# Output projection of an attention block: twelve of sixteen token tiles by Strassen's seven block products

## The reference, cut to what matters

```python
x = L0_attn_hidden_states                       # 4 x 512 tokens, 1024 channels
xn = _layernorm(x, axis=-1)
s = _L0_attn_ref(xn, Wq, Wk, Wv, Wo)            # 16 heads of 64, causal; its last line:
#   return out @ Wo                             #   out: 2048 x 1024, Wo: 1024 x 1024
g = _silu(_L0_ffn_ref(xn, weight, bias, gate_w, in_channel_scale, out_channel_scale))
x = x + s * g                                   # what is returned
```

## Time and profile before

| What | Value |
|---|---|
| Median of 3 runs | 1167.71 us (1166.72 to 1168.52) |
| The profiled execution: its own time | 1166.3 us |
| Its span, from the first to the last instruction | 1164.5 us |
| Mean granted TensorE clock | 0.994 |
| PE busy over the span | 1132.8 us (97%) |
| Wo's matmuls of tiles 4 to 15 | 12 x 48 = 576, about from 1028 to 1159 us |

### The profile page before, as it was taken

One profiled execution on the slowest core, in us unless ns is written; L12 is line 12 of the kernel. 1 busy time (PEld: TensorE's weight loads), 2 busy tenths in 40 slices (PEclk: granted clock), 3 DMA queues, 4 the chain that ended last, 5 costly groups with the idle time before them and its releaser, 6 DMA issues.

```text
span 1164.5 us, 17720 instructions
## 1 busy us (share of the span) xinstructions
PE 1132.8 (97%) x5692; PEld 945.4 (81%) x5692; DVE 727.5 (62%) x1731; ACT 611.7 (53%) x1286; POOL 424.5 (36%) x254
## 2 busy tenths in 40 slices
PE   4899999999999999999999999999999999999998
PEld 3677777788888888888888888888888887888886
DVE  6757741477767777677676776767767678323222
ACT  6545543266655666656665566655666577312211
POOL 0433537343342433424334252342523434222221
PEclk9899999999999999999999999999999999999999
DMA  9425132220202202022360220202202034565662
GB/s 368 192 91 235 55 91 109 73 64 10 63 9 72 63 9 63 9 72 63 144 216 9 72 63 9 63 9 72 63 9 63 9 112 168 172 204 179 193 207 99
DMA packets 87271, 112.01 MB, mean 96 GB/s; under 512 B 3408, under 2 KB 68944, under 8 KB 86224
## 3 DMA queue, kind: packets, MB, share of 16 engines
q1 hardware_dynamic: 87248, 111.72, 28.9%
HBM read 78.15 MB, written 33.55 MB: 96 GB/s over the span
## 4 chain that ended last, share of the span: by engine, by line
PE 88%; DVE 6%; ACT 2%; issue 1%; POOL 1%; DMA 1%; SPq 0%; DVEq 0%; POOLq 0%; ACTq 0%
PE at_proj L44 17%; PE at_proj L46 17%; PE at_proj L45 17%; PE at_out L978 7%; PE ff_z_ps L287 6%; PE at_pt L965 6%; PE at_score L947 3%; PE at_score L948 3%; PE at_score L44 3%; PE at_score L46 2%; PE at_score L45 2%; POOL ff_xs_lo L679 1%; PE at_proj L932 1%; DVE xs_full L600 1%; DMA z<-fn_in_channel_scale_dram 1%
## 5 line engine op out<-in xcount | busy, mean ns | idle before, releaser
L44 PE MATMUL at_proj<-xn_hi,w_hi 128*128 128x512 f32 x896 | 361.7, 404 | 1.6 <-POOL w_lo L1403 0.8
L46 PE MATMUL at_proj<-xn_hi,w_lo 128*128 128x512 f32 x896 | 350.9, 392 | 0.0
L45 PE MATMUL at_proj<-xn_lo,w_hi 128*128 128x512 f32 x896 | 349.4, 390 | 0.0
L46 PEld LDWEIGHTS at_proj<-xn_hi,w_lo 128*128 128x128 f32 x896 | 168.2, 188 | 37.3
L44 PEld LDWEIGHTS at_proj<-xn_hi,w_hi 128*128 128x128 f32 x896 | 168.5, 188 | 31.9 <-issue 1.2
L45 PEld LDWEIGHTS at_proj<-xn_lo,w_hi 128*128 128x128 f32 x896 | 168.8, 188 | 30.3
L1387 POOL TENSOR_TENSOR at_turning<-at_turning,rope_table 128x512 f32<-128x512 f32 x64 | 82.9, 1295 | 289.3 <-DVE at_turning L1231 289.3
L1395 POOL TENSOR_TENSOR w_lo<-w_stage,w_hi 128x1024 fp32r<-128x1024 f32 x45 | 114.4, 2557 | 162.9 <-ACT w_hi L1063 162.9
L1101 ACT ACTIVATE at_prob<-at_score,at_neg_max 128x512 f32<-128x512 f32 (+3 forms) x256 | 133.3, 526 | 71.2 <-DVE at_neg_max L1259 70.8
L1110 ACT ACTIVATE at_pt_hi<-at_pt 128x512 fp32r<-128x512 f32 (+1 forms) x192 | 94.0, 524 | 99.9 <-PE at_pt L965 99.1
L1276 DVE TENSOR_TENSOR at_pt_lo<-at_pt,at_pt_hi 128x512 fp32r<-128x512 f32 (+1 forms) x192 | 111.9, 597 | 42.2 <-ACT at_pt_hi L1110 41.2
(11 more groups left out here) (125 smaller groups left out, 1825.6 us busy)
## 6 DMA issues: line engine op xcount, KB each, us to landing
z_store<-z SPq DMA_DIRECT2D x16, 512.0 KB, 2.7
w_stage<-in_L_attn_Wq_dram SPq DMA_DIRECT2D x16, 512.0 KB, 3.8
w_stage<-in_L_attn_Wk_dram SPq DMA_DIRECT2D x16, 512.0 KB, 5.1
w_stage<-in_L_attn_Wv_dram SPq DMA_DIRECT2D x16, 512.0 KB, 6.2
att_store<-at_att_t SPq DMA_DIRECT2D x32, 256.0 KB, 2.0
rope_table<-att_store SPq DMA_DIRECT2D x16, 512.0 KB, 6.7
z<-_attn_hidden_states_dram SPq DMA_DIRECT2D x16, 512.0 KB, 5.0
at_turning<-z_store SPq DMA_DIRECT2D x16, 512.0 KB, 6.1
```

The costliest lines, as they stand in the source:

```text
L44: pe.matmul(out, sh, mh, start=first, stop=False)
L45: pe.matmul(out, sh, ml, start=False, stop=False)
L46: return pe.matmul(out, sl, mh, start=False, stop=final)
```

## The change

Tiles 0 to 3 stay as they are (`PLAIN = 4`). Tiles 4 to 15 are taken in six rounds of two tiles. In a round the two tiles' attention rows are a 2 x 2 matrix of blocks (A11, A12 from the even tile, A21, A22 from the odd one, each 128 tokens by 512 channels), and Wo is one as well (512 by 512 each). Seven block products, each of 4 x 3 = 12 matmuls, give the four output blocks, by way of sums: S1 = A21 + A22, S2 = S1 - A11, S3 = A11 - A21, S4 = A12 - S2 on the side of attention, and T1 to T4 of Wo's blocks. That is 84 matmuls in a round, where two tiles had 96.

What comes with it:

- **Before the rounds**: Wo is loaded a second time (`load_rows`, four loads of two rows of blocks, 512 KB each), DVE makes T1 to T4 from it (`sums`, 16 instructions), ACT makes high parts (`sums_high`, 16), DVE and POOL low parts (`sums_low`, 8 each).
- **In each round**: DVE makes the four sums of attention blocks (`row_sums`) and four low parts (`op_low`), POOL three low parts, ACT seven high parts (`op_hi`), all of 128x512. ACT copies a partial sum out of PSUM three times (`part_copy`), because bank a goes on accumulating for another output block; DVE adds three banks to those copies (`block_sum`), multiplies and adds x by halves (`block_out`, three times two), and `block_21` ends the round with the last product's bank.
- **Order**: TensorE's products in a round are P1 = A11 W11 (bank a), P2 = A12 W21 (bank b), P3 = S2 T2 (a), P4 = S1 T1 (c), P5 = S3 T3 (a), P6 = S4 W22 (c), P7 = A22 T4 (a). P3 waits for the copy of P1's bank, P5 for that of P3's, P6 for that of P4's, and P7 for `block_sum(q, 2)`, which reads bank a after P5. The next round has other banks.
- **Buffers**: the result is written over x (four places, `x_slots`), no longer into `y_tile`; the multiplication writes over z. `load_z` and `load_x` are apart, and the loads of z and of attention rows stand ahead of the next store in SP's queue.

The core of the diff:

```diff
+        sum_b = sb("at_sum_b", [P, 2, EMBED], F32)
+        wo_sum = [[sb(f"at_wo_sum{t}_{part}", [P, QT, HALF], F32R) for part in ("hi", "lo")] for t in range(4)]
+        a22 = sb("at_a22", [P, 2, HALF], F32R)
+        partial = sb("at_partial", [P, 3, HALF], F32)
...
-        x_tile = keep["z"]
+        x_slots = [keep["z"][:, p, :] for p in range(2)] + [keep["w_stage"][:, p, :] for p in range(2)]
         z_tile = turning[:].rearrange("p a b n -> p a (b n)")
-        y_tile = [prob[p][:, 0:EMBED] for p in range(2)]
+
+        wo_rows = [sum_b, keep["w_stage"][:, 0:2, :]]
+        att_sum = sum_b[:].rearrange("p a (b n) -> p (a b) n", b=2)
...
+        banks = [(pt_ps[0], pt_ps[1], out_ps), (proj_ps[0], proj_ps[1], score_ps[0])]
...
+            def load_rows(k):
+
+                if k == 0:
+                    sp.wait_ge(qk_ready, 2 * STEPS)
+                    sp.wait_ge(v_tr, STEPS)
+                    sp.wait_ge(scored, 6 * STEPS - 6)
+                elif k == 1:
+                    wait_wo(sp, 6)
+                    wait_wo(sp, 7)
+                else:
+                    sp.wait_ge(sum_low_dve, 2 * (k - 1))
+                    sp.wait_ge(sum_low_pool, 2 * (k - 1))
+                for half in range(2):
+                    rows = slice((QT * half + k) * P, (QT * half + k + 1) * P)
+                    sp.dma_start(wo_rows[k % 2][:, half, :], io["wo"][rows, :]).then_inc(rows_in[k % 2], 16)
...
+            load_rows(2)
+            store_y(0)
+            load_z(2)
+            load_att(4)
+            store_y(1)
+            load_z(3)
+            load_x(2)
+            load_x(3)
+            load_rows(3)
...
+            for n in range(PLAIN, TILES, 2):
+                store_y(n)
                 if n + 2 < TILES:
-                    load_att(n + 2)
-                sp.wait_ge(y_add, n + 1)
-                sp.dma_start(out[tile_rows(n), :], y_tile[n % 2]).then_inc(y_out[n % 2], 16)
+                    load_z(n + 2)
+                if n + 4 < TILES:
+                    load_att(n + 4)
+                    load_att(n + 5)
+                store_y(n + 1)
                 if n + 2 < TILES:
-                    load_xz(n + 2)
+                    load_z(n + 3)
+                if n + 4 < TILES:
+                    load_x(n + 4)
+                    load_x(n + 5)
...
+            def product(out, op, moving, first):
+                (sh, sl), (mh, ml) = operand(op), moving
+                for k in range(QT):
+                    last = split_matmuls(pe, out[:], (sh[:, k, :], sl[:, k, :]), (mh[k], ml[k]), first=(first and k == 0),
+                                         final=(k == QT - 1), reopened=not first)
+                last.then_inc(product_done, 1)
...
+                product(a, A11, wo_block(0, 0), True)
+                pe.wait_ge(op_low_pool, 3 * q + 2)
+                product(b, A12, wo_block(1, 0), True)
+                pe.wait_ge(op_low_dve, 4 * q + 1)
+                pe.wait_ge(sum_low_dve, 2 * QT - 1)
+                pe.wait_ge(partial_ok, 3 * q + 1)
+                product(a, S2, wo_sum_block(T2), False)
+                pe.wait_ge(op_low_dve, 4 * q + 2)
+                pe.wait_ge(sum_low_dve, 2 * QT)
+                product(c, S1, wo_sum_block(T1), True)
+                pe.wait_ge(op_low_dve, 4 * q + 3)
+                pe.wait_ge(sum_low_pool, 2 * QT - 1)
+                pe.wait_ge(partial_ok, 3 * q + 2)
+                product(a, S3, wo_sum_block(T3), False)
+                pe.wait_ge(op_low_dve, 4 * q + 4)
+                pe.wait_ge(partial_ok, 3 * q + 3)
+                product(c, S4, wo_block(1, 1), False)
+                pe.wait_ge(op_low_pool, 3 * q + 3)
+                pe.wait_ge(sum_low_pool, 2 * QT)
+                pe.wait_ge(block_read, 3 * q + 2)
+                product(a, A22, wo_sum_block(T4), False)
...
+            def part_copy(q, which):
+
+                act.wait_ge(product_done, 7 * q + (1, 3, 4)[which])
+                if q >= 1:
+                    act.wait_ge(block_done, 3 * (q - 1) + (1, 3, 2)[which])
+                act.activation(partial[:, which, :], banks[q % 2][(0, 0, 2)[which]][:], ACT.Copy).then_inc(partial_ok, 1)
...
+            op_hi(0, A11)
+            op_hi(0, A12)
+            sums_high(3)
+            silu(3, 1)
+            for op in (S2, S1, S3, S4, A22):
+                op_hi(0, op)
+            for q in range(ROUNDS_W):
+                n = PLAIN + 2 * q
+                more = q + 1 < ROUNDS_W
+                part_copy(q, 0)
+                part_copy(q, 1)
+                silu(n, 0)
+                part_copy(q, 2)
+                if more:
+                    op_hi(q + 1, A11)
+                    op_hi(q + 1, A12)
+                silu(n + 1, 1)
+                if more:
+                    for op in (S2, S1, S3, S4, A22):
+                        op_hi(q + 1, op)
...
+            sums(3)
+            sums_low(3)
+            row_sums(0)
+            op_low(0, S2)
+            op_low(0, S1)
+            gate(3, 1)
+            op_low(0, S3)
+            op_low(0, S4)
+            for q in range(ROUNDS_W):
+                more = q + 1 < ROUNDS_W
+                block_sum(q, 0)
+                if more:
+                    row_sums(q + 1)
+                    op_low(q + 1, S2)
+                block_sum(q, 2)
+                if more:
+                    op_low(q + 1, S1)
+                block_out(q, 0, 0, 0, False)
+                block_out(q, 2, 1, 1, False)
+                if more:
+                    op_low(q + 1, S3)
+                block_sum(q, 1)
+                block_out(q, 1, 0, 1, True)
+                if more:
+                    op_low(q + 1, S4)
+                block_21(q)
```

More of the change, by code:

```diff
@@ L739, in attention_block @@
         turned = [turning[:, 1, c, :] for c in range(2)]
[L740 to L748, removed]
@@ L799, in attention_block, with x_slot, x_tile, wait_x @@
         TILES = BATCH * QT
+        PLAIN = 4
+        ROUNDS_W = (TILES - PLAIN) // 2
+        A11, A12, S2, S1, S3, S4, A22 = range(7)
+        T1, T2, T3, T4 = range(4)
+        SUM_ORDER = (S1, S3, S2, S4)
+        def x_slot(n):
+            return 2 * (n >= PLAIN and n // 2 % 2 == 0) + n % 2
+        def x_tile(n):
+            return x_slots[x_slot(n)]
+        def wait_x(engine, n):
+            engine.wait_ge(x_in[x_slot(n)], 16 * sum(x_slot(i) == x_slot(n) for i in range(n + 1)))
+        def operand(op):
+            if op == A22:
+                return [a22[:, part, :].rearrange("p (k n) -> p k n", k=QT) for part in range(2)]
+            pair, half = ((2, 0), (2, 1), (0, 0), (0, 1), (1, 0), (1, 1))[op]
+            return [w[pair][:, QT * half:QT * (half + 1), :] for w in (w_hi, w_lo)]
+        def att_rows(op):
+            tile, half = {A11: (0, 0), A12: (0, 1), A22: (1, 1)}[op]
+            return att_raw[:, tile, half * HALF:(half + 1) * HALF]
+        def flat(ap):
+            return ap.rearrange("p k n -> p (k n)")
         def wait_wo(engine, k):
@@ L1376, in _ @@
             merge(s - 1, 2 * s - 1, 1, 1)
+            sums(0)
             gate(0, 0)
+            sums_low(0)
+            sums(1)
+            sums_low(1)
             gate(1, 1)
-            with dve.Fori(1, TILES // 2) as i:
-                for p in range(2):
-                    gate(2 * i + p, p)
+            sums(2)
+            sums_low(2)
+            gate(2, 0)
+            sums(3)
[6 more added lines that the diff above has]
+            op_low(0, S4)
+            for q in range(ROUNDS_W):
+                more = q + 1 < ROUNDS_W
[15 more added lines that the diff above has]
+                block_21(q)
         @block.gpsimd
@@ L1442, in _, with sums_low, op_low @@
             att_lo(1, 1)
-            with pool.Fori(1, TILES // 2) as i:
-                for p in range(2):
-                    att_lo(2 * i + p, p)
+            def sums_low(k):
+                for count, (t, half) in enumerate(((T3, 0), (T4, 1))):
+                    pool.wait_ge(wo_sum_high, 4 * k + count + 3)
+                    pool.tensor_tensor(wo_sum[t][PLO][:, k, :], wo_rows[k % 2][:, half, 0:HALF], raw(wo_sum[t][PHI][:, k, :]),
+                                       ALU.subtract).then_inc(sum_low_pool, 1)
+            def op_low(q, op):
+                pool.wait_ge(op_high, 7 * q + op + 1)
+                hi, lo = operand(op)
+                pool.tensor_tensor(flat(lo), att_rows(op), raw(flat(hi)), ALU.subtract).then_inc(op_low_pool, 1)
+            sums_low(0)
+            att_lo(2, 0)
+            sums_low(1)
+            att_lo(3, 1)
+            sums_low(2)
+            op_low(0, A11)
+            op_low(0, A12)
+            sums_low(3)
+            op_low(0, A22)
+            for q in range(1, ROUNDS_W):
+                op_low(q, A11)
+                op_low(q, A12)
+                op_low(q, A22)
 def later(count, least):
```

212 lines of the change are left out of this document (178 added, 34 removed).

## The result

The changed kernel took 1171.29 us (median of 17 runs, 1169.95 to 1176.81), the one before 1167.12 us on the same chip (17 runs, 1166.23 to 1168.78): a ratio of 1.0036, 95% interval 1.0027 to 1.0045. So the kernel has 72 matmuls fewer and takes 4.2 us more; 1171.5 was predicted. The profiled execution took 1173.31 us, 2.0 above the median, with a span of 1171.5.

The account below looks back on a forecast made before the run. PE, busy 97%, was taken as the bound. On the profiled 1166.3 us: -16.3 - 1.2 + 2.0 + 7.6 + 2.7 + 4 x 2.25 = +3.8, giving 1170.1; median 1.4 above: 1171.5, range 1160 to 1177.

Parts of the forecast that it names:

- Matmuls and tail, -17.5: 72 matmuls fewer in the six rounds, 16.3 us less, and shorter work after the last matmul, 1.2 us less.
- the upper end of 4 us: Cost of reopening banks already read: nothing taken, at most 42 products x 0.09 = 4 us.
- Tile 2, 2.0 us: Entry: PE waits 2 us ahead of tile 2 for POOL's low part of its rows.
- P7 of round 0, 2.7: First round: P7 waits 2.7 us more, row_sums(1) standing ahead of block_sum(0, 2).
- P3 of round 0, 7.6: First round: P3 waits 7.6 us for ACT's copy of P1's bank, a chain starting at tile 1's store.
- 1028.3: Entry: time when the second half of load_rows(3), sixth transfer of its batch, lands, 1017.1 + 11.2.
- POOL's low part of A11 keeps DVE until 1029.2: Entry: this POOL part holds DVE until 1029.2 us, before sums(3) takes 3.9 us.
- P7 in rounds 1 to 4, 2.25 each: A round's chain takes 21.3 us against PE's 19.04, so PE waits 2.25 us ahead of each P7.
- the third step: End of a round's chain: ACT's Silu and S2 high part, DVE's low part and block_sum, four handovers: 3.2 us.
- the two chains "of equal length": In each round, odd z's landing and the attention rows, some 3 us earlier, then row_sums, end at about the same time.
- The rival on the other side: Rounds: transfers and DVE keep up, PE is the bound again, only the entry's waits remain; 1159.8 us, chance 0.17.
- The clock: Slow matmuls after PE's waits lose 1.5 to 1.7 us a drop; nothing counted in rounds 0 to 3.

Follow-up runs that it names:

- e10_no_waits: Changed kernel without Wo's sums (output not the reference's), attention loads ahead of the even store, round 0's block_sum(0, 2) ahead of row_sums(1): 1150.35 us.
- e6_copy_first: Changed kernel with ACT's copy of P1's bank ahead of the five high parts of the first round's sums: 1169.97 us.
- e1_s2_first: Changed kernel with ACT making the next round's high parts of S2 and S1 ahead of the odd tile's Silu: 1171.16 us.
- e2_rows_first: Changed kernel with both attention loads ahead of the even tile's store and z in SP's queue: 1163.79 us.
- u1_stores_first: Changed kernel with SP issuing both tiles' stores ahead of the loads: 1178.84 us.
- e8_read_round0: Changed kernel with attention loads ahead of the even store, P1's bank copy ahead of round 0's high parts, block_sum(0, 2) ahead of row_sums(1): 1160.26 us.
- e4_no_wo_sums: Changed kernel without Wo's second load and T1 to T4, plain blocks of Wo instead (output not the reference's): 1161.16 us.
- e7_rows_copy: Changed kernel with attention loads ahead of the even store and P1's bank copy ahead of round 0's high parts: 1161.02 us.

## Why the prediction was right, step by step

- **Matmuls and tail, -17.5**: right; `e10_no_waits` measures -16.9, with 0.8 us of small waits in it. Banks that are taken up again cost nothing that shows, so the upper end of 4 us for them is out.
- **Tile 2, 2.0 us**: 1.6. **P7 of round 0, 2.7**: 2.3.
- **P3 of round 0, 7.6**: 5.2, with slow matmuls behind it for which the sum has nothing. The term was sized too long in two steps. "1028.3": Wo's last rows had landed when `sums(3)` began, at 1026.91. And "POOL's low part of A11 keeps DVE until 1029.2": that part was all but over, and the next one, A12's, ran beside `sums(3)` from 1027.16 and is in the 3.9 us counted for it (measured 3.86). So `part_copy(0, 0)` came at 1039.47, not at 1042.6. P7 of round 0 came at 1055.95, where 1056.9 was forecast: what P3 gained was lost again to the slow matmuls (7.6 + 2.7 counted for both waits; 5.2 + 2.5 + 2.3 measured with them). That P3 waited for this copy, at the end of ACT's row of six, is what `e6_copy_first` shows.
- **P7 in rounds 1 to 4, 2.25 each**: 2.3, 2.3, 2.2 and 2.3. Its pieces hold too, though the third step adds up to 3.4 us (1.06 + 0.6 + 0.65 + 0.65 + 0.4), not 3.2, so that the three give 21.6 where 21.3 was taken and 21.44 measured. DVE's twelve instructions took 8.5 us (1077.16 to 1085.65), and z landed 11.55 us after the batch's first issue (11.6). The 326 GB/s behind that figure is no ceiling: within the batch, slices of 0.6 us moved up to 413 GB/s. Of the two chains "of equal length" I put z first; it is the rows, by 0.3 us, and not 3 us earlier than z but 2.4. That an earlier z alone wouldn't help is what `e1_s2_first` shows; `e2_rows_first` shows that the rows are the handle (-7.5), `u1_stores_first` points the same way (+7.6). That this is just 4 x 1.9 is partly luck: its rounds are 22.9 us on average, 1.5 longer, and the rest is elsewhere.
- **The rival on the other side** (PE bound again, 1159.8) is a state that the kernel can reach, but not by the order of two loads alone: with it the kernel takes 1163.8, and with three edits of order (`e8_read_round0`) 1160.3. That this is so near to 1159.8 is no confirmation of the sum, since P3's wait is 3.1 us there and 7.6 in the sum.
- **The clock.** Behind P3's wait of 5.0 us matmuls began 0.43 us apart instead of 0.23 in every trace that had it, but behind P7's 2.1 us only in rounds 2 and 4 of five. The Trainium skill, "TensorE: Matmul & The Clock Gate", Part 1, has an idle engine go back to half its clock; the trace agrees for the long wait, and my "probably" for those of 2.2 us came true in two of five. In rounds 0 to 3 I counted nothing for it, as P7's next wait would take it up: so it was in `e6_copy_first` (0.39 left of 2.13) and once in `e4_no_wo_sums` (0.42). Behind P3 it held in part: the slow matmuls shortened P7's wait (2.3 us, against 4.2 in `e6_copy_first`, which had none of them), but P7 also came later.
- **Round 3** took 22.99 us in the changed kernel's profiled execution, since its rows began to be summed 10.9 us behind the batch's first issue, against 9.2 and 9.0 in the two rounds before. Their loads were issued as far behind that first issue as ever (0.9 and 1.7 us), so the transfers themselves took longer. Whether that has to do with the clock is open; in `e6_copy_first` and `e4_no_wo_sums` the round behind a drop took 21.27 and 21.35 us. The longer round is part of why this execution is above the median. The drop in round 4 has nothing to cover it (1.5 us).
- **The sum** for that execution, from its rows: -17.5, waits 1.6 + 5.2 + 5 x 2.3, some 2.5 of slow matmuls behind P3, 1.5 in round 4 and 1.5 in round 2: +6.3, where the span grew by 7.0. The forecast's +3.8 had P3 2.4 too long and nothing for the slow matmuls behind it, which cancel, and nothing for the 3.0 in rounds 2 and 4. The median of the runs is 2.0 below this execution, a change of +4.2, and no trace shows which drops it had; so the closeness of 1171.5 to 1171.29 is partly luck. The round, which decides the sign, was not.

## What to carry to other kernels

When arithmetic is taken off the bounding engine, ask how long one round's chain is through the other engines and the queue, not how busy they are: DVE was busy 13 of 20 us here, the DMA engines 0.64 of the time, and the round was still 2.3 us too long. Then look at what stands ahead of the transfer that ends last: a store, with its wait for the tile's result, and a z in front of the attention rows were worth 7.5 us, more than the whole loss. Shortening the chain that isn't the latest shows nothing, even where it is only 0.3 us behind.

## What the runs showed of the hardware

- **An issue can take 3 us itself.** SyncE's odd store lasted 3.09 us in the row at 1064.94 (2.84 to 3.30 in the next three rounds), where issues took 0.34 to 0.79 before. It is the fifth transfer of a batch; the odd z behind it is issued late by as much, in 0.43 us again, and the next load, an x, takes 1.20 at 1068.55. A row of several issues can hide a wait: the one of both loads of x covers 4.38 us, of which 2.85 lie between them, until the odd store has landed.
- **The same wait does or doesn't cost the clock.** `e7_rows_copy` and `e8_read_round0` both wait 3.1 us ahead of P3; the windows behind it:

```profile
1040.00:1042.00 2.00, 2.00 (x6) 1.52 (x6) 1.97 (x2) 0.00 (x0) 1.28 (x1) 0.50 0.87 265
```

of the first, and of the second:

```profile
1042.00:1043.00 1.00, 1.00 (x6) 0.83 (x5) 0.97 (x3) 0.43 (x1) 0.50 (x1) 1.00 0.82 269
```

The granted clock is 0.50 (1.2 GHz) in the one and 1.00 (2.4 GHz) in the other, where it stays 1.00 from P3 to 1060 us. Before the change the runs lay within 2.6 us, after it within 6.9. The slowest (1176.81) has the lowest granted clock of its 17 runs, 0.985, but one with 0.988 took 1170.19: that the drops make this spread is plausible, and not shown.
